# Moving the feed-forward weights' preparation and reordering the attention turns' seams in a fused transformer layer

## The chip, the cores and the metric

One core of one Trainium2 chip runs the whole program. The metric is device time in microseconds, taken as the median of the runs. The engines named below are TensorE (PE, matrix products), VectorE (DVE), ScalarE (ACT), GpSimd (POOL) and SyncE (SP, which issues most transfers). Each engine works through its own queue strictly in the order in which the program writes it, and waits on semaphores that other engines raise.

## The reference

```python
h = _layernorm(x) * (1 + ca) + sa            # x: (2, 1024, 256)
# 4 key/value heads, 4 query heads each, D = 128, causal
scores = einsum('bsgqd,btgd->bgqst', q, k) * scale
attn = softmax(where(causal, scores, -big))
x = x + ga * (einsum('bgqst,btgd->bsgqd', attn, v).reshape(b, s, NH*D) @ wproj)
h = _layernorm(x) * (1 + cb) + sb
h = fwht(h * SU_ug) / 64                     # Walsh-Hadamard transform, 256 wide
h = silu(h @ W_gate.T * g) * (h @ W_up.T * u)    # 1024 wide
x = x + gb * (fwht(h * SU_dp) / 64 @ W_down.T * d)
```

Everything is float32. The modulations (sa, ca, ga, sb, cb, gb) come from a small product of the conditioning vector.

## The kernel before

A float32 product is made of three reduced-precision products: each operand is split into a high part (rounded) and a low part (the rest), and `three()` issues high x high, high x low and low x high. So every operand needs a copy (the high part) and a subtraction (the low part) on ACT, DVE or POOL before PE may use it.

**Attention** runs in 8 turns t, one for each pair of batch and key/value head. The order of all work in it is one list, `WALK`, which every engine walks through, each taking its own share of each item:

- `C`: a chunk of the next turn's query, key or value projection; `S i h`: the scores of row block i (128 queries) and head part h, with the maximum on DVE, the exponential on ACT and the normalisation on POOL.
- `T n`: four transposes of unit n (a row block and a block of 128 keys), then the high part `pt_hi` on ACT and the low part `pt_lo` on DVE; `V n`: the product with the values, two units behind its T (`LAG`). After the last V of a row block ACT and DVE take `o_hi` and `o_lo` from the sum.
- `Y i`: the output projection of row block i (12 products), which DVE adds to x. `VS`: ACT and DVE split the next turn's values (`v_hi`, `v_lo`, two instructions each). `WP`: POOL splits the projection weights. `L`: PE transposes the second layer norm's input of two row blocks, with `LF`, `LN` before and `LH`, `LL` behind it.

Row blocks are worked in windows of a big and a small one: (7,0), (6,1), (5,2), (4,3). `UNITS` begins each window with three units (`HEAD`) of the big block, then takes the small one, then the rest of the big one. The **seam** is the stretch from turn t's last units to turn t+1's first transposes. Score tiles live in two pairs of PSUM banks, S[0] for h = 0 and 2, S[1] for h = 1 and 3. The scores of blocks 4 to 7 take a whole pair, so the wait ahead of them in PE's S branch (L1210 and L1211) is for the exponential of two score items earlier. The exponentials on ACT are put off by `exps()`: a score item's exponential is issued at ACT's next S, T, L or VS item. PE's two rotating transpose banks (`ring`) hold T and L tiles alike.

**The feed-forward part** folds the Walsh-Hadamard transforms into the weights. Six pieces, in the order `PIECES = [0, 1, 4, 5, 2, 3]` (0 to 3 up and gate, 4 and 5 down), each pass through: a sum and a difference on POOL (`last_butterfly`), a high part (`raw_hi`), a low part on POOL (`raw_lo`), four products with a Hadamard matrix `had_r` on PE (`P n`), and a high and a low part of the result on ACT and DVE (`weights_high`, `weights_low`). `split_piece(n)` does all POOL has to do of piece n at once. `B 2` in the last turn is piece 0; the others follow WALK. `FIRST` orders the first chunk of 512 rows: `G m` is gate and up product m (12 products), its silu, its product with the up half (`g32`) and the split into `g_hi` and `g_lo`; `D m` is the down product (12 products); `L n` a layer norm step. The other three chunks run in a loop.

Of the kernel before, what the change touches and what calls it, by code (L numbers as in the profile page):

```python
# [5 lines left out]
F32 = mybir.dt.float32  # L6
# [30 lines left out]
HEAD = 3  # L37
UNITS = []
for big, small in WINDOWS:
    UNITS += [(big, j) for j in range(HEAD)] + [(small, j) for j in range(small + 1)] + [(big, j) for j in range(HEAD, big + 1)]  # L40
# [33 lines left out]
def walk():  # L74
# [15 lines left out]
    for t in range(TURNS):  # L90
        s0, s6 = scores(t, 0), scores(t, NT - 2)
        rest = [(t - 1, "Y", i, 0) for i in WINDOWS[-1][::-1]] if t else []
        out += rest[:1] + [(t, "VS", 0, 0)] + s0[3 if t else 0:] + ([s6[0]] if t else []) + rest[1:]
# [13 lines left out]
        for p, pair in enumerate(WINDOWS):  # L107
# [64 lines left out]
def build(nc, x_in, wqkv, wv, wproj, wmod, c_cols, wug, wdn, su_ug, su_dp, ws_ug, ws_dp, ident_in, mask_in, had_in, out):  # L172
    ctx = ExitStack()
    with ctx:
# [337 lines left out]
        def _(pool):  # L512
# [67 lines left out]
            def split_piece(n):  # L580


                last_butterfly(PIECES[n])
                if n == 1:
                    pool.wait_ge(s_done, this(s_done, TURNS - 1, 32))
                if n < 4:
                    pool.wait_ge(last_fly_s, n + 1)
                    for k, z in enumerate(halves_of(PIECES[n])):
                        last = g_.tensor_scalar(raw_hi[n][:, k, :], z, 1.0, 1.0, ALU.mult, ALU.mult)
                    last.then_inc(rhi_s, 1)  # L590
# [33 lines left out]
            for t, what, n, h in WALK:  # L624
# [25 lines left out]
                if what == "B" and n == 2:  # L650
                    split_piece(0)
# [5 lines left out]
            for n in range(1, len(PIECES)):  # L657
                split_piece(n)
# [8 lines left out]
        def _(act):  # L667
# [94 lines left out]
            for t, what, n, h in WALK:  # L762
# [37 lines left out]
            def gated_high(m):  # L800

                act.wait_ge(g32_s, m + 3)
                a_.activation(g_hi[:, g_slot(m), :], g32[:, m % 2, :], ACT.Copy).then_inc(ghi_s, 1)

            for what, n in FIRST:
                if what == "P":
                    weights_high(n)
                if what == "P" and n in (2, 3):
                    raw_high(n + 2)
                if what == "G":  # L810
                    gate(0, n)
                    gated_high(n)
                if what == "L":
# [7 lines left out]
        def _(dve):  # L821
# [153 lines left out]
            for t, what, n, h in WALK:  # L975
# [394 lines left out]
```

## Time and profile before

| what | value |
|---|---|
| median of 3 runs | 945.65 us (945.41 to 945.97) |
| the profiled execution | 945.19 us, of which its span is 943.0 us |
| PE busy | 911.5 us, 97% of the span |
| DVE, ACT, POOL busy | 632.1, 511.3, 488.0 us |
| granted TensorE clock | 0.998 of full speed |
| PE, DVE, ACT, POOL over 820 to 900 us | 79.98, 45.36, 19.44, 6.56 us busy |

The span ends with the last store; the 2.2 us that the profiled execution has beyond it lie around it. Times in a timeline are from the span's start. A PE row is marked busy until its modelled end, which overlaps the next row: products of 512 columns follow one another 0.23 us apart though each is marked 0.39. So the start of one row to the start of the next is the safer measure of a wait.

### The profile page before, as it was taken

The page shows a single profiled execution, that of the slowest core. Times are in us where ns is not written, and L with a number is a line of the kernel's source. Part 1 is how long each engine was busy: PE and PEld are TensorE (multiplying, and loading weights), DVE is VectorE, ACT ScalarE, POOL GpSimd, SP SyncE. Part 2 cuts the span into 40 slices and gives each one's busy share as a digit, 9 for nine tenths or more (in the row PEclk, how much of TensorE's full clock was granted, in tenths as well). Part 3 has the DMA queues.
Part 4 walks back from the last instruction along what each step waited for, and adds up shares of the span by engine and source line. Part 5 has one row for each costly group of instructions (what it writes and reads, how often), then busy time and mean ns, then how long its engine had stood idle before and what let it go on. Part 6 is the DMA issues. An engine that isn't in the chain of part 4 may idle for free.

```text
span 943.0 us, 15013 instructions
## 1 busy us (share of the span) xinstructions
PE 911.5 (97%) x5480; PEld 805.4 (85%) x5480; DVE 632.1 (67%) x1299; ACT 511.3 (54%) x1113; POOL 488.0 (52%) x705
## 2 busy tenths in 40 slices
PE   5989999999999999999999999999999998899997
PEld 4878888888888888888888888888888987788886
DVE  6567757764787578747875787478757875664554
ACT  3366656654766476647664666476647664531111
POOL 2276718570767186707671867076717989420000
PEclk9999999999999999999999999999999999999999
DMA  7000100000001000000010000000001001000000
GB/s 278 23 1 1 41 1 23 1 28 1 23 1 40 1 23 1 28 1 23 2 40 1 23 1 29 2 17 7 1 1 68 1 30 45 1 12 11 22 22 23
DMA packets 10180, 21.21 MB, mean 22 GB/s; under 512 B 1280, under 2 KB 5760, under 8 KB 9984
## 3 DMA queue, kind: packets, MB, share of 16 engines
q1 hardware_dynamic: 9392, 20.11, 6.3%
q8 instruction: 41, 0.67, 0.3%
q10 hardware_dynamic: 720, 0.21, 0.1%
q14 instruction: 27, 0.22, 0.1%
HBM read 18.22 MB, written 2.10 MB: 22 GB/s over the span
## 4 chain that ended last, share of the span: by engine, by line
PE 71%; DVE 14%; ACT 7%; POOL 5%; issue 2%; DMA 1%; SPq 0%; DVEq 0%; POOLq 0%
PE ps L1089 16%; PE ps L1091 16%; PE ps L1090 16%; PE ps L1238 8%; DVE ps L1012 5%; PE ps L1227 5%; PE ps L1224 4%; PE ps L1221 4%; ACT prob L757 4%; DVE pt_lo L1016 3%; ACT pt_hi L782 2%; DVE stats L855 1%; DVE xhat L871 1%; PE ps L1113 1%; DVE vare L863 1%
## 5 line engine op out<-in xcount | busy, mean ns | idle before, releaser
L617 POOL TENSOR_TENSOR rinv<-rsum,mone 128x1 f32<-128x1 f32 x256 | 144.7, 565 | 243.3 <-ACT prob L757 243.3
L1016 DVE TENSOR_TENSOR pt_lo<-ps,pt_hi 128x512 fp32r<-128x512 f32 x288 | 198.0, 688 | 65.9 <-ACT pt_hi L782 62.8
L782 ACT ACTIVATE pt_hi<-ps 128x512 fp32r<-128x512 f32 x288 | 171.1, 597 | 126.5 <-PE ps L1238 126.0
L757 ACT ACTIVATE prob<-ps,nmax 128x256 f32<-128x256 f32 (+28 forms) x256 | 180.7, 706 | 85.2 <-DVE nmax L1012 84.2
L1012 DVE CUSTOM_DVE_ANT_0 ps<-ps,mask_f 128x256 f32<-128x256 f32 (+28 forms) x256 | 182.7, 719 | 46.8 <-PE ps L1227 44.7
L622 POOL TENSOR_SCALAR prob<-prob,rinv 128x256 f32<-128x256 f32 (+28 forms) x256 | 183.0, 715 | 38.2 <-POOL rinv L617 38.2
L1238 PE MATMUL ps<-ident,prob 128*128 128x128 f32 x1152 | 173.1, 273 | 4.5 <-POOL prob L622 2.7
L1238 PEld LDWEIGHTS ps<-ident,prob 128*128 128x128 f32 x1152 | 141.1, 141 | 23.5 <-DVE pt_lo L1016 3.7
L1089 PE MATMUL ps<-pt_hi,v_hi 128*128 128x512 f32 x288 | 134.5, 467 | 2.1 <-DVE pt_lo L1016 2.1
L1091 PE MATMUL ps<-pt_hi,v_lo 128*128 128x512 f32 x288 | 113.7, 395 | 0.0
L1090 PE MATMUL ps<-pt_lo,v_hi 128*128 128x512 f32 x288 | 113.5, 394 | 0.0
L1221 PE MATMUL ps<-k_hi,q_hi 128*128 128x256 f32 (+16 forms) x352 | 99.8, 343 | 0.6
L1227 PE MATMUL ps<-k_hi,q_lo 128*128 128x256 f32 (+16 forms) x352 | 98.0, 337 | 0.0
L1224 PE MATMUL ps<-k_lo,q_hi 128*128 128x256 f32 (+16 forms) x352 | 97.7, 337 | 0.0
L949 DVE SCALAR_TENSOR_TENSOR q_lo<-ps,q_hi 128x512 fp32r<-128x512 f32 x64 | 44.1, 691 | 55.4 <-ACT q_hi L722 55.4
L1221 PEld LDWEIGHTS ps<-k_hi,q_hi 128*128 128x128 f32 x352 | 62.9, 189 | 14.3 <-ACT prob L757 3.8
L1089 PE MATMUL ps<-wp_hi,o_hi 128*128 128x256 f32 x256 | 72.6, 284 | 0.0
L1091 PE MATMUL ps<-wp_hi,o_lo 128*128 128x256 f32 x256 | 72.4, 283 | 0.0
L1090 PE MATMUL ps<-wp_lo,o_hi 128*128 128x256 f32 x256 | 72.2, 282 | 0.0
L797 ACT ACTIVATE prob<-ps,ws_u 128x512 f32<-128x512 f32 x32 | 22.0, 688 | 86.8 <-PE ps L1091 86.8
L1224 PEld LDWEIGHTS ps<-k_lo,q_hi 128*128 128x128 f32 x352 | 63.9, 189 | 5.7
L1089 PE MATMUL ps<-h_hi,w_hi 128*128 128x512 f32 x160 | 66.0, 412 | 2.9 <-DVE h_lo L886 2.9
(173 smaller groups left out, 1794.9 us busy)
## 6 DMA issues: line engine op xcount, KB each, us to landing
w_raw<-in_wqkv SPq DMA_DIRECT2D x8, 640.0 KB, 3.9
wp_raw<-in_wproj SPq DMA_DIRECT2D x8, 512.0 KB, 3.4
out_y<-prob SPq DMA_DIRECT2D x8, 256.0 KB, 2.3
x<-in_x SPq DMA_DIRECT2D x3, 512.0 KB, 12.6
prob<-in_wug SPq DMA_DIRECT2D x3, 512.0 KB, 4.2
prob<-in_wmod SPq DMA_DIRECT2D x1, 1024.0 KB, 10.0
wv_raw<-in_wv SPq DMA_DIRECT2D x4, 256.0 KB, 4.4
raw_down<-in_wdn SPq DMA_DIRECT2D x1, 1024.0 KB, 4.8
```

The costliest lines, as they stand in the source:

```text
L622: g_.tensor_scalar(row(i, h), row(i, h), rinv[:, at, h:h + 1], 1.0, ALU.mult, ALU.mult).then_inc(prob_done, 1)
L757: a_.activation(row(i, h).rearrange("p (a n) -> p a n", a=nb), score_banks(i, h).rearrange("p (a n) -> p a n", a=nb)[:, :, 0:w], ACT.Exp, ...
L782: a_.activation(pt_hi[:, n % 3, :], ring(t, "T", n), ACT.Copy).then_inc(pth_done, 1)
L1012: v_.tensor_tensor_reduce(scores, scores, late, -1.0, 3.0e38, ALU.add, ALU.min, nmax[:, place(n), h:h + 1]).then_inc(max_done, 1)
L1016: v_.tensor_tensor(pt_lo[:, n % 3, :], ring(t, "T", n), pt_hi[:, n % 3, :].bitcast(F32), ALU.subtract).then_inc(ptl_done, 1)
L1089: mm(dst, w_h, r_h, start=start, stop=False)
L1090: mm(dst, w_h, r_l, start=False, stop=False)
L1091: return mm(dst, w_l, r_h, start=False, stop=stop)
L1221: mm(dst[:, a * CH:a * CH + wide], queries(q_hi, n, h), k_hi[:, a * w:a * w + wide], start=True, stop=False)
L1224: mm(dst[:, a * CH:a * CH + wide], queries(q_hi, n, h), k_lo[:, a * w:a * w + wide], start=False, stop=False)
L1227: last = mm(dst[:, a * CH:a * CH + wide], queries(q_lo, n, h), k_hi[:, a * w:a * w + wide], start=False, stop=True)
L1238: last = tr(ring(t, "T", n)[:, q * P:(q + 1) * P], row(i, q, j * P, (j + 1) * P), ident[:, :])
```

## The change

1. **Unit order and seams.** `HEADS` replaces HEAD: the last window begins with two units of block 4 instead of three, so block 3's last unit is unit 32 and no longer 33. `Y 3` (t) comes before S 0 1, S 0 2 (t+1) and V 35, and `Y 4` moves behind S 6 1, right before T 0. `L` moves behind the V item that followed it. On ACT two calls of exps() are left out, so that the exponential of S 7 3 goes behind pt_hi of unit 35.
2. **End of the last turn.** POOL does sums of later pieces ahead of low parts of earlier ones, and only the high part of piece 0 stays with it: ACT takes those of pieces 1, 2 and 3. The two Hadamard matrices' rounding moves from DVE to ACT. Both P 0 and P 1 come before Y 4.
3. **First chunk.** D m comes one gate later (behind G m+2), the splits of g32 get items `R` of their own, and g_hi, g_lo rotate over three slots.

```diff
-HEAD = 3
+HEADS = [3, 3, 3, 2]
...
-        rest = [(t - 1, "Y", i, 0) for i in WINDOWS[-1][::-1]] if t else []
-        out += rest[:1] + [(t, "VS", 0, 0)] + s0[3 if t else 0:] + ([s6[0]] if t else []) + rest[1:]
+        rest = [(t - 1, "Y", WINDOWS[-1][0], 0)] if t else []
+        out += [(t, "VS", 0, 0)] + s0[3 if t else 0:] + ([s6[0]] if t else [])
...
-                out += extra[:1] + [(t, "T", n, 0)] + extra[1:]
+                transposes = [item for item in extra if item[1] == "L"]
+                extra = [item for item in extra if item[1] != "L"]
+                out += extra[:1] + (rest if n == 0 else []) + [(t, "T", n, 0)] + extra[1:]
                 behind.append(n)
                 if len(behind) > LAG:
                     value()
+                out += transposes
...
-    for n, i in enumerate(WINDOWS[-1][::-1]):
-        out += [(TURNS - 1, "Y", i, 0), (TURNS - 1, "P", n, 0)]
+    out += [(TURNS - 1, "P", 0, 0), (TURNS - 1, "P", 1, 0), (TURNS - 1, "Y", WINDOWS[-1][0], 0)]
...
-FIRST = [("G", 0), ("P", 2), ("G", 1), ("D", 0), ("P", 3), ("G", 2), ("D", 1), ("P", 4), ("G", 3),
-         ("D", 2), ("P", 5), ("G", 4), ("D", 3), ("L", 0), ("G", 5), ("D", 4), ("L", 1), ("G", 6), ("D", 5), ("L", 2),
-         ("G", 7), ("L", 3), ("D", 6)]
+FIRST = [("G", 0), ("P", 2), ("R", 0), ("G", 1), ("P", 3), ("R", 1), ("G", 2), ("R", 2), ("D", 0), ("P", 4), ("G", 3), ("R", 3),
+         ("D", 1), ("P", 5), ("D", 2), ("G", 4), ("R", 4), ("D", 3), ("L", 0), ("G", 5), ("R", 5), ("D", 4), ("L", 1),
+         ("G", 6), ("R", 6), ("D", 5), ("L", 2), ("G", 7), ("R", 7), ("L", 3), ("D", 6)]
...
-            for n in range(1, len(PIECES)):
-                split_piece(n)
+            raw_low_part(0)
+            last_butterfly(PIECES[1])
+            last_butterfly(PIECES[2])
+            raw_low_part(1)
+            last_butterfly(PIECES[3])
+            raw_low_part(2)
+            raw_low_part(3)
+            last_butterfly(PIECES[4])
+            last_butterfly(PIECES[5])
+            raw_low_part(4)
+            raw_low_part(5)
...
                 if what == "S":
-                    exps()
+                    if not (t and n == h == 0):
+                        exps()
                     waiting.append((t, n, h))
...
-                    exps()
+                    if n != NU - 2:
+                        exps()
+                    if t == TURNS - 1 and n in (NU - 4, NU - 3):
+                        raw_high(1, n - NU + 4)
+                if what == "H":
+                    act.wait_ge(had_s, 16)
+                    for a in range(2):
+                        last = a_.activation(had_r[a], had_f[:, a, :], ACT.Copy)
+                    last.then_inc(consts, 1)
                 if what == "P":
                     weights_high(n)
+                    if n == 1:
+                        raw_high(3)
...
+                    if t == TURNS - 1 and n == NU - 1:
+                        raw_high(2)
```

What the queues hold, in the order in which the instructions stand, with the semaphores they wait for. First ACT's queue at a seam, before: from the exponential of S 7 3 (1024 wide) to that of S 0 3 (128 wide); 32, 64, 96 and 128 columns are S 0 0 to S 0 3.

```order
L757 ACTIVATE prob,rsum<-ps,nmax 128x1024 [waits max_done]
L782 ACTIVATE pt_hi<-ps 128x512 [waits transposed]
L757 ACTIVATE prob,rsum<-ps,nmax 128x32 [waits max_done]
L789 ACTIVATE o_hi<-ps 128x512 [waits pv_done]
L757 ACTIVATE prob,rsum<-ps,nmax 128x64 [waits max_done]
L789 ACTIVATE o_hi<-ps 128x512 [waits pv_done]
L757 ACTIVATE prob,rsum<-ps,nmax 128x96 [waits max_done]
L704 ACTIVATE v_hi<-raw_down 128x512 [waits pv_done,v_raw_done]
L704 ACTIVATE v_hi<-raw_down 128x512
L757 ACTIVATE prob,rsum<-ps,nmax 128x128 [waits max_done]
```

And the same place now:

```order
L816 ACTIVATE o_hi<-ps 128x512 [waits pv_done]
L799 ACTIVATE pt_hi<-ps 128x512 [waits transposed]
L773 ACTIVATE prob,rsum<-ps,nmax 128x1024 [waits max_done]
L773 ACTIVATE prob,rsum<-ps,nmax 128x32 [waits max_done]
L773 ACTIVATE prob,rsum<-ps,nmax 128x64 [waits max_done]
L816 ACTIVATE o_hi<-ps 128x512 [waits pv_done]
L773 ACTIVATE prob,rsum<-ps,nmax 128x96 [waits max_done]
L716 ACTIVATE v_hi<-raw_down 128x512 [waits pv_done,v_raw_done]
L716 ACTIVATE v_hi<-raw_down 128x512
L773 ACTIVATE prob,rsum<-ps,nmax 128x128 [waits max_done]
```

The first `o_hi` (block 3) and a `pt_hi` moved ahead of the 1024-wide exponential. The exponential of S 0 2 (96) still stands behind `o_hi` of block 4, which waits for V 35, and that of S 0 3 (128) behind both `v_hi`.

PE's queue at the same seam, before, from S 0 1 to the first transpose of the next turn (`wp_hi,o_hi` is a Y item, `pt_hi,v_hi` a V item; the first row of each is shown, "..." stands for its others):

```order
L1217 MATMUL ps<-k_first,q_first 128x64 [waits first_row_done,exp_done]
L1217 MATMUL ps<-k_first,q_first 128x96 [waits first_row_done,exp_done]
L1089 MATMUL ps<-pt_hi,v_hi 128x512 [waits pt_lo_done]
...
L1089 MATMUL ps<-wp_hi,o_hi 128x256 [waits o_lo_done]
...
L1217 MATMUL ps<-k_first,q_first 128x128 [waits first_row_done,exp_done]
L1221 MATMUL ps<-k_hi,q_hi 128x400 [waits exp_done]
...
L1089 MATMUL ps<-wp_hi,o_hi 128x256 [waits o_lo_done]
...
L1221 MATMUL ps<-k_hi,q_hi 128x416 [waits exp_done]
...
L1238 MATMUL ps<-ident,prob 128x128 [waits prob_done,pt_lo_done]
```

And now:

```order
L1124 MATMUL ps<-pt_hi,v_hi 128x512 [waits pt_lo_done]
...
L1124 MATMUL ps<-wp_hi,o_hi 128x256 [waits o_lo_done]
...
L1252 MATMUL ps<-k_first,q_first 128x64 [waits first_row_done,exp_done]
L1252 MATMUL ps<-k_first,q_first 128x96 [waits first_row_done,exp_done]
L1124 MATMUL ps<-pt_hi,v_hi 128x512 [waits pt_lo_done]
...
L1252 MATMUL ps<-k_first,q_first 128x128 [waits first_row_done,exp_done]
L1256 MATMUL ps<-k_hi,q_hi 128x400 [waits exp_done]
...
L1256 MATMUL ps<-k_hi,q_hi 128x416 [waits exp_done]
...
L1124 MATMUL ps<-wp_hi,o_hi 128x256 [waits o_lo_done]
...
L1273 MATMUL ps<-ident,prob 128x128 [waits prob_done,pt_lo_done]
```

Y 3 moved from between V 35 and S 0 3 (128x128) to ahead of S 0 1, and Y 4 from between S 6 0 (400) and S 6 1 (416) to behind both.

DVE's queue at the same seam now holds, from the addition of Y 3 on, the maxima (ISA), `o_lo` and the values' low parts:

```order
L1051 TENSOR_TENSOR x<-ps,x 128x256 [waits y_done]
L1037 ISA ps,nmax<-ps,mask_f 128x64 [waits scores_done]
L1037 ISA nmax 128x1
L1037 ISA ps,nmax<-ps,mask_f 128x96 [waits scores_done]
L1037 ISA nmax 128x1
L1046 TENSOR_TENSOR o_lo<-ps,o_hi 128x512 [waits o_hi_done]
L985 TENSOR_TENSOR v_lo<-raw_down,v_hi 128x512 [waits v_hi_done] x2
L1037 ISA ps,nmax<-ps,mask_f 128x128 [waits scores_done]
L1037 ISA nmax 128x1
L1037 ISA ps,nmax<-ps,mask_f 128x2x400 [waits scores_done]
L1037 ISA nmax 128x1
```

The addition of Y 3 stands ahead of the maxima of S 0 1 and S 0 2, where it used to stand behind `o_lo`; the maximum of S 0 3 stands behind both `v_lo`, as before.

Last, ACT's queue at the end of the last turn, from unit 29's high part to the first weights' high parts (`su_u`), before:

```order
L782 ACTIVATE pt_hi<-ps 128x512 [waits transposed] x7
L789 ACTIVATE o_hi<-ps 128x512 [waits pv_done] x2
L730 ACTIVATE q_hi<-ps,su_u 128x512 [waits hadamard_done] x4
```

And now:

```order
L799 ACTIVATE pt_hi<-ps 128x512 [waits transposed] x3
L807 ACTIVATE had_r<-prob 128x128 [waits had_loaded]
L807 ACTIVATE had_r<-prob 128x128
L799 ACTIVATE pt_hi<-ps 128x512 [waits transposed]
L760 ACTIVATE k_hi<-dif_down 128x512 [waits scores_done,last_butterflies]
L799 ACTIVATE pt_hi<-ps 128x512 [waits transposed]
L760 ACTIVATE k_hi<-prob 128x512 [waits scores_done,last_butterflies]
L799 ACTIVATE pt_hi<-ps 128x512 [waits transposed]
L816 ACTIVATE o_hi<-ps 128x512 [waits pv_done]
L799 ACTIVATE pt_hi<-ps 128x512 [waits transposed]
L816 ACTIVATE o_hi<-ps 128x512 [waits pv_done]
L760 ACTIVATE q_hi<-sum_down 128x512 [waits last_butterflies]
L760 ACTIVATE q_hi<-raw_down 128x512
L742 ACTIVATE q_hi<-ps,su_u 128x512 [waits hadamard_done] x4
```

ACT's queue gained the two `had_r` rows (from DVE), and `k_hi` and `q_hi` of pieces 1 and 2 (from POOL). The last two `q_hi` rows stand ahead of the four weights' rows for which the first gate product waits.

## Rows read from the trace of the kernel before

**Rows 1.** The page: busy times by engine, and one costly group (busy, mean ns, idle).

```profile
PE 911.5 (97%) x5480; PEld 805.4 (85%) x5480; DVE 632.1 (67%) x1299; ACT 511.3 (54%) x1113; POOL 488.0 (52%) x705
...
L617 POOL TENSOR_TENSOR rinv<-rsum,mone 128x1 f32<-128x1 f32 x256 | 144.7, 565 | 243.3 <-ACT prob L757 243.3
```

**Rows 2.** PE's waits: who was waited for, total us, times, longest.

```profile
PE ps L1113 <- DVE pt_lo L1016: 2.3, 8, 0.3
PE ps L1089 <- DVE pt_lo L1016: 2.1, 7, 0.4
```

**Rows 3.** Timeline of PE at turn 6's seam: start, us, operation.

```profile
713.68 0.58 PE L1217 MATMUL ps<-k_first,q_first 128*128 128x64 f32 x4
...
714.54 0.50 PE L1089 MATMUL ps<-pt_hi,v_hi 128*128 128x512 f32 x1 [0.28 <-DVE pt_lo L1016]
...
715.34 0.34 PE L1089 MATMUL ps<-wp_hi,o_hi 128*128 128x256 f32 x1
...
716.98 0.60 PE L1221 MATMUL ps<-k_hi,q_hi 128*128 128x400 f32 x2
...
718.15 0.28 PE L1089 MATMUL ps<-wp_hi,o_hi 128*128 128x256 f32 x1
...
719.58 0.54 PE L1221 MATMUL ps<-k_hi,q_hi 128*128 128x416 f32 x2
...
720.71 0.60 PE L1238 MATMUL ps<-ident,prob 128*128 128x128 f32 x4
```

**Rows 4.** Timeline of ACT at the same seam.

```profile
715.77 0.59 ACT L789 ACTIVATE o_hi<-ps 128x512 fp32r<-128x512 f32 x1
716.25 0.34 ACT L757 ACTIVATE prob<-ps,nmax 128x96 f32<-128x96 f32 x1
...
716.57 1.16 ACT L704 ACTIVATE v_hi<-raw_down 128x512 fp32r<-128x512 f32 x2
718.96 0.37 ACT L757 ACTIVATE prob<-ps,nmax 128x128 f32<-128x128 f32 x1 [1.24 <-DVE nmax L1012]
719.23 0.19 ACT L757 ACTIVATION_READ_ACCUMULATOR prob<-ps,nmax 128x1 f32 x1
```

**Rows 5.** Timeline of DVE at the same seam.

```profile
717.38 1.28 DVE L955 TENSOR_TENSOR v_lo<-raw_down,v_hi 128x512 fp32r<-128x512 f32 x2
...
718.58 0.29 DVE L1012 CUSTOM_DVE_ANT_0 ps<-ps,mask_f 128x128 f32<-128x128 f32 x1
```

**Rows 6.** Timeline of POOL at the same seam.

```profile
717.43 1.04 POOL L617 TENSOR_TENSOR rinv<-rsum,mone 128x1 f32<-128x1 f32 x1
```

**Rows 7.** Timeline of PE around item L of turn 6.

```profile
655.33 0.60 PE L1238 MATMUL ps<-ident,prob 128*128 128x128 f32 x4
...
656.23 0.66 PE L1113 MATMUL ps<-ident,xhat 128*128 128x128 f32 x4 [0.30 <-DVE pt_lo L1016]
...
657.90 0.60 PE L1238 MATMUL ps<-ident,prob 128*128 128x128 f32 x4
```

**Rows 8.** Timeline of DVE at that place.

```profile
656.77 0.69 DVE L1016 TENSOR_TENSOR pt_lo<-ps,pt_hi 128x512 fp32r<-128x512 f32 x1
```

**Rows 9.** Timeline of PE, last turn and first chunk: the four long waits.

```profile
778.97 0.33 PE L1238 MATMUL ps<-ident,prob 128*128 128x128 f32 x1 [1.09 <-POOL prob L622]
...
786.14 0.66 PE L1238 MATMUL ps<-ident,prob 128*128 128x128 f32 x4 [1.31 <-DVE pt_lo L1016]
...
802.88 0.39 PE L1089 MATMUL ps<-k_hi,pt_hi 128*128 128x256 f32 x1 [1.50 <-DVE v_lo L970]
...
820.01 0.39 PE L1089 MATMUL ps<-k_hi,pt_hi 128*128 128x256 f32 x1 [1.61 <-DVE pt_lo L1037]
```

**Rows 10.** Timeline of POOL in the last turn.

```profile
772.05 1.29 POOL L593 TENSOR_TENSOR w_lo<-dif_down,w_hi 128x512 fp32r<-128x512 f32 x1
```

**Rows 11.** Timeline of DVE in the last turn.

```profile
783.14 2.34 DVE L989 CAST had_r<-prob 128x128 fp32r<-128x128 f32 x2
```

**Rows 12.** Timeline of ACT: the first weights' high parts.

```profile
792.25 1.27 ACT L730 ACTIVATE q_hi<-ps,su_u 128x512 fp32r<-128x512 f32 x2 [1.31 <-PE ps L1188]
```

More of the change, by code:

```diff
@@ L36 @@
 WINDOWS = [(NT - 1 - p, p) for p in range(NW)]
-HEAD = 3
+HEADS = [3, 3, 3, 2]
 UNITS = []
-for big, small in WINDOWS:
-    UNITS += [(big, j) for j in range(HEAD)] + [(small, j) for j in range(small + 1)] + [(big, j) for j in range(HEAD, big + 1)]
+for (big, small), ahead in zip(WINDOWS, HEADS):
+    UNITS += [(big, j) for j in range(ahead)] + [(small, j) for j in range(small + 1)] + [(big, j) for j in range(ahead, big + 1)]
 NU = len(UNITS)
@@ L142, in walk @@
             value()
-        assert [i for _, i in due] == list(WINDOWS[-1][::-1])
-    for n, i in enumerate(WINDOWS[-1][::-1]):
-        out += [(TURNS - 1, "Y", i, 0), (TURNS - 1, "P", n, 0)]
+        assert [i for _, i in due] == [WINDOWS[-1][0]]
+    out += [(TURNS - 1, "P", 0, 0), (TURNS - 1, "P", 1, 0), (TURNS - 1, "Y", WINDOWS[-1][0], 0)]
     return out
@@ L578, in last_butterfly, with first_high, raw_low_part @@
                 g_.tensor_tensor(b, a, b, ALU.subtract).then_inc(last_fly_s, 1)
[L580 to L590, printed above, removed]
+            def first_high():
+                pool.wait_ge(last_fly_s, 1)
+                for k, z in enumerate(halves_of(PIECES[0])):
+                    last = g_.tensor_scalar(raw_hi[0][:, k, :], z, 1.0, 1.0, ALU.mult, ALU.mult)
+                last.then_inc(rhi_s, 1)
+            def raw_low_part(n):
                 pool.wait_ge(rhi_s, n + 1)
@@ L737, in weights_high, with raw_high @@
                         last.then_inc(fhi_s, 1)
-            def raw_high(n):
+            def raw_high(n, only=None):
                 act.wait_ge(last_fly_s, n + 1)
+                if n == 1:
+                    act.wait_ge(s_done, this(s_done, TURNS - 1, 32))
                 if n == 4:
@@ L744, in raw_high @@
                 for k, z in enumerate(halves_of(PIECES[n])):
-                    last = a_.activation(raw_hi[n][:, k, :], z, ACT.Copy)
-                last.then_inc(rhi_s, 1)
+                    if only in (None, k):
+                        last = a_.activation(raw_hi[n][:, k, :], z, ACT.Copy)
+                if only != 0:
+                    last.then_inc(rhi_s, 1)
             waiting = []
@@ L807, in _ @@
                     weights_high(n)
-                if what == "P" and n in (2, 3):
-                    raw_high(n + 2)
                 if what == "G":
                     gate(0, n)
+                if what == "R":
                     gated_high(n)
+                    if n < 2:
+                        raw_high(n + 4)
                 if what == "L":
@@ L985, in _ @@
                         ln_low(0, 0, 1, slot)
-                if what == "H":
-                    dve.wait_ge(had_s, 16)
-                    for a in range(2):
-                        last = v_.tensor_copy(had_r[a], had_f[:, a, :])
-                    last.then_inc(consts, 1)
                 if what == "G":
@@ L1032, in gated, with gated_high, gated_low, product @@
                                         ALU.mult, ALU.mult).then_inc(g32_s, 1)
+            def gated_high(c, m):
                 dve.wait_ge(g32_s, c * NM + m + 3)
[L1034 to L1035 removed]
+                v_.tensor_copy(g_hi[:, g_slot(m), :], g32[:, m % 2, :]).then_inc(ghi_s, 1)
+            def gated_low(c, m, first=False):
                 dve.wait_ge(ghi_s, c * NM + m + 1)
[L1037 removed]
+                v_.tensor_tensor(g_lo[:, g_slot(m, first), :], g32[:, m % 2, :], g_hi[:, g_slot(m, first), :].bitcast(F32),
                                  ALU.subtract).then_inc(g_ok, 1)
+            def product(c, m):
+                gated(c, m)
+                gated_high(c, m)
+                gated_low(c, m)
             def scale_out(c):
@@ L1061, in _ @@
                 if what == "G":
-                    gated(0, n, False)
+                    gated(0, n)
+                if what == "R":
+                    gated_low(0, n, True)
                 if what == "L":
@@ L1069, in _ @@
             with dve.Fori(1, B * NC_B) as c:
-                gated(c, 0)
+                product(c, 0)
                 scale_out(c - 1)
-                gated(c, 1)
+                product(c, 1)
                 finish(c - 1)
                 for m in range(2, NM):
-                    gated(c, m)
+                    product(c, m)
             scale_out(B * NC_B - 1)
@@ L1281, in gate_up, with down @@
                 last.then_inc(gu_s, 1)
-            def down(c, m):
+            def down(c, m, first=False):
                 if m == 0:
@@ L1308, in _ @@
                         pe.wait_ge(wf_ok, KH * (PIECES.index(4 + n // 2) + 1))
-                    down(0, n)
+                    down(0, n, True)
                 if what == "L":
```

19 lines of the change are left out of this document (10 added, 9 removed).

## The prediction

> **What bounds the kernel now.** The page first: PE is busy 911.5 us, 97% of the span [rows 1]. Whatever helps another engine counts only where PE waits for it, so I read next who PE waits for. Apart from the start and the last store there are few places. Two come in every turn: the transposes of item L wait for `pt_lo` (8 times, 2.3 us together), and the value product V 35 at the seam waits for it (7 times, 2.1 us) [rows 2]. Four come once, at the end of the last turn and in the first chunk: 1.09 us for POOL's scores, 1.31 for `pt_lo`, 1.50 for `v_lo`, 1.61 for the low part of g [rows 9]. With the tails that are marked busy ahead of them (0.15 to 0.35 each) the four are 6.3 us; a fifth of 0.19 (no row here) makes it 6.5. So the most that the change can win, if it removes all of it and adds nothing, is 6.5 us there, 8 x 0.54 at L, and 7 x 0.6 at the seam: about 15 us. What it costs depends on the waits that it lays bare, so each place has to be walked through with PE's starts.
>
> **The seams.** In turn 6's seam PE starts S 0 1 at 713.68, V 35 at 714.54, Y 3 at 715.34, S 6 0 at 716.98, Y 4 at 718.15, S 6 1 at 719.58 and T 0 at 720.71 [rows 3]. Without a wait S 0 1 and S 0 2 would take 0.28 (their row is marked 0.58, of which some 0.3 is tail), so V 35 lost 0.58 there. The pieces of work are then, start to start: V 35 0.80, Y 3 1.50, S 0 3 0.14 (together 1.64 up to S 6 0), S 6 0 1.17, Y 4 1.43, S 6 1 1.13.
>
> Now put them in the new order, from the same 713.68. Y 3 runs to 715.18 (its `o_lo` is early, since block 3 ends one unit sooner), S 0 1 and S 0 2 to 715.46, V 35 to 716.26 without its wait, S 0 3 to 716.40. S 6 0 must have the exponential of S 0 2. On ACT that stands behind `o_hi` of block 4, which needs V 35. Before, `o_hi` began at 715.77, 0.43 after V 35, but behind another exponential; alone I take 0.20 (between nothing and 0.43). Then, from ACT's starts [rows 4], 0.48 for `o_hi` and 0.32 for the exponential with a tail of 0.1 until it is seen. That is 716.26 + 0.20 + 0.48 + 0.42 = 717.36 to 717.4. So S 6 0 waits 1.0 us where it used to wait for nothing: Y 3, which stood between V 35 and it, is gone.
>
> S 6 1 needs the exponential of S 0 3. It stands behind both `v_hi`, and its maximum behind both `v_lo`. From the first `v_hi` (716.57) to that exponential (718.96) took 2.39, and it ended 0.46 later at 719.42 [rows 4]. DVE's two `v_lo` (717.38) and the maximum (718.58) lie inside it [rows 5]. Of the 2.39 a part was `v_lo` beginning 0.2 late behind Y 3's addition, which now comes earlier, so I take 2.2 to 2.39. The new `v_hi` begins at 717.26, so the exponential ends at 719.9 to 720.1 and S 6 1 starts at about 720.0. S 6 0 was done at 717.4 + 1.17 = 718.57: a wait of 1.4 us. In the kernel before, 1.43 us of Y 4 lay exactly there, and S 6 1 began 0.16 after the exponential's end [rows 3, 4]. Now Y 4 comes behind S 6 1 and T 0 starts at 720.0 + 1.13 + 1.43 = 722.56 instead of 720.71. **Each seam loses 1.85 us, seven of them 13.0.** Check by waits: 1.0 + 1.4 new, 0.58 gone. Bounds: 1.6 (no latency after V 35, 2.2) to 2.1 (0.43, 2.39). The exponential of S 7 3, now behind `pt_hi` of unit 35, ends some 0.8 us later; S 0 1, which needs it, starts 1.5 later than it did, so this costs nothing.
>
> **Item L.** The transposes end at 655.69 (655.33 and 0.36) and L begins at 656.23, 0.54 late [rows 7]. With V 12 (0.77) between them L no longer waits. The next transposes (657.90) need unit 14's `pt_lo`, which ends at 656.77 + 0.69 = 657.46 and does not depend on L [rows 7, 8]. They can move up only to 657.5. So 0.38 of the 0.54 is won, 8 x 0.38 = 3.1 us (bounds 2.4 and 4.3).
>
> **The end of the last turn and the first chunk.** Term by term:
> - The 1.09 (1.44 with its tail): the transposes of block 3 wait for the scores' normalisation, behind four instructions of piece 0. The two of the low part take 2.5 us from 772.05 on [rows 9, 10] and move behind. The same transposes come 1.13 us earlier. 0.1 is left: 1.3 won.
> - The 1.31 (1.48): DVE rounds the Hadamard matrices in 2.34 us from 783.14 on, ahead of a `pt_lo` [rows 9, 11]. On ACT they lie in a gap of some 0.9 us. No row shows this copy on ACT; it is no more than the 512 wide `v_hi` (0.58 each) [rows 4], so 0.4 to 1.2 us, hidden but for at most 0.3. All of it is won. But block 3's first value product now follows block 5's projection by one transposes item (0.35) and shares its bank, so it waits for an addition on DVE: 0.2 + 0.42 + 0.06 less 0.35 = 0.33 lost.
> - POOL's new order delivers piece 1's sums at 781.4, and ACT takes its halves between two `pt_hi`. No wait of PE follows.
> - The first gate product needs the weights of piece 0. ACT now does both halves of piece 2 (about 1.05) before their high parts, which take 1.27 [rows 12], then 0.7 for the last low part. PE reaches the product 0.65 before that: 0.65 lost.
> - The 1.50 and 1.61 (3.4 with tails): down product 0 now stands behind gate 2, 3.6 us more of cover, and D 3 has its g one gate earlier on PE's side. The layer norm's 4.1 us on DVE still stand before g 3, but begin 5 us sooner. 0.25 is left.
>
> 6.5 less 0.1, 0.33, 0.65 and 0.25 is 5.2 us won (bounds 4.0 and 6.5). From 820 us on PE was full and stays so.
>
> **A rule against it.** DVE's two `v_lo` read two SBUF tensors each. While they ran, POOL's one-column reciprocal took 1.04 us, where its mean is 0.565 [rows 1, 6]. The Trainium skill (SBUF — State Buffer, "SBUF: two separate sides") says that GpSimd and a VectorE instruction with two SBUF inputs take a shared port pair in turn, and that whichever comes second is fully blocked. By that rule, the trace agrees. Before, the second `v_lo` came first; in the new seam POOL's scores of S 0 2 fall due just before it, and if POOL is first the chain to S 6 1 grows by up to 0.5 us, seen from the 0.48 by which that reciprocal was longer. I leave it out of the sum and keep it as a rival.
>
> **The sum**, against the profiled execution's 945.19 us: + 13.0 - 3.1 - 5.2 = + 4.7, so 949.9. The median of the runs lies 0.46 above that execution; I say 950.0. Own range: + 11.2 - 4.3 - 6.5 = + 0.4 to + 14.7 - 2.4 - 4.0 = + 8.3, that is 946.0 to 954.0 on the median's scale.
>
> **The rivals.**
> - *Forecast, slower by 3 to 8 us:* 0.62.
> - *POOL is first at the shared port:* 7 x 0.5 more, about 953.5. For it the 1.04 us; against it, the two start within a tenth of each other, so either may win. 0.13.
> - *The seams' waits are as costed at the low end and the other gains at the high end, or one of the waits is smaller by 0.5 us:* within 0.2% (1.9 us, about what a measurement of this kernel can tell from no change) of before. 0.13.
> - *Faster:* the seam is not bound by ACT's queue, S 6 0 and S 6 1 find their exponentials done, and the 0.58 of V 35 is won: 945.65 - 4.1 - 3.1 - 5.2 = 933.3. For it, that Y 3 ahead of S 0 1 is just what removes the one wait that the seam shows [rows 3]. Against it, both queues in order: the exponential of S 0 2 can't pass `o_hi`, nor that of S 0 3 the `v_hi`. The point that decides is a seam that loses under (3.1 + 5.2) / 7 = 1.2 us. 0.12.
>
> Range, with the near parts of the neighbouring cases: 945.0 to 954.5. Slower by over 0.2% (above 947.5): 0.77; within 0.2%: 0.12; faster: 0.11.
>
> **What would show it.** In the new trace: S 6 0 (400 columns) and S 6 1 (416) each preceded by an idle PE released by ACT's `prob`, about 0.8 and 1.2 us idle, seven times, and no wait at the 128x64 score rows or V 35; L's transposes without one; from the end of V 35 to T 0 6.3 us instead of 5.4. In the last turn, the four long waits gone, and ones of about 0.3 and 0.65 before the first value product of block 3 and the first gate product. I am wrong if the seam is short (then the first part of this text failed), or if ACT in the last turn holds up `pt_hi` behind a sum that POOL has not finished.

## The result and the profile after

The changed kernel takes **957.87 us** (median of 4 runs, 957.75 to 958.36) against 945.81 for the kernel before on the same chip: ratio 1.0126, 95% interval 1.0113 to 1.0139. The forecast was 950.0 with a range up to 954.5. It has the direction and is off by 8 us in size. The profiled execution took 957.75 (span 955.9, against 943.0). The mean granted clock was 0.988 to 0.991 in all four executions, where those of the kernel before that are on record with a clock have 0.995 to 0.998.

The page after, the lines that answer to [rows 1], and the granted clock's line:

```profile
PE 918.4 (96%) x5480; PEld 811.3 (85%) x5480; DVE 629.8 (66%) x1297; ACT 516.6 (54%) x1121; POOL 489.7 (51%) x699
...
PEclk9999999999999999999999999999999999999999
```

PE is *busier* by 6.9 us with the same 5480 matmuls. So the loss is not idle time alone: some products took longer. The clock's line hides why, since a slice is 24 us and a digit 9 stands for anything from 90% up. PE's waits after (who was waited for, total us, times, longest):

```profile
PE ps L1256 <- ACT prob L773: 14.3, 14, 1.3
...
PE ps L1222 <- POOL w_lo L595: 0.7, 1, 0.7
PE ps L1124 <- issue: 0.5, 1, 0.5
PE ps L1124 <- DVE o_lo L1046: 0.2, 1, 0.2
```

L1256 is the first product of a score block. It waits for ACT's exponentials 14 times, twice in each of seven seams. The waits of [rows 2] and the four of [rows 9] are gone; the wait of 0.2 for `o_lo` is one of turn 1 alone. PE at turn 6's seam, answering to [rows 3]:

```profile
729.55 0.58 PE L1252 MATMUL ps<-k_first,q_first 128*128 128x64 f32 x4
729.91 0.47 PE L1124 MATMUL ps<-pt_hi,v_hi 128*128 128x512 f32 x1
...
731.86 0.45 PE L1256 MATMUL ps<-k_hi,q_hi 128*128 128x400 f32 x1 [0.79 <-ACT prob L773]
...
734.47 1.06 PE L1256 MATMUL ps<-k_hi,q_hi 128*128 128x416 f32 x2 [1.25 <-ACT prob L773]
735.33 0.89 PE L1259 MATMUL ps<-k_lo,q_hi 128*128 128x416 f32 x2
736.02 0.90 PE L1262 MATMUL ps<-k_hi,q_lo 128*128 128x416 f32 x2
736.72 0.41 PE L1124 MATMUL ps<-wp_hi,o_hi 128*128 128x256 f32 x1
736.93 0.42 PE L1125 MATMUL ps<-wp_lo,o_hi 128*128 128x256 f32 x1
...
738.68 0.60 PE L1273 MATMUL ps<-ident,prob 128*128 128x128 f32 x4
```

Up to the start of S 6 1 this is the forecast seam: V 35 without a wait, S 6 0 1.95 us after V 35, S 6 1 2.61 behind it. Then it is not. S 6 1's next two groups begin 0.86 and 0.69 later; at full clock the block's three groups take 1.13 in all [rows 3]. Y 4's products stand 0.21 apart instead of 0.12 (1.43 for twelve), until 737.9. The windows of PE (span, busy and count, granted clock, DMA share, GB/s) show it in turn 1's seam, which is built alike:

```profile
249.00:251.00 2.00, 1.15 (x3) 0.70 0.00 0
251.00:253.00 2.00, 2.00 (x9) 0.50 0.00 0
253.00:255.00 2.00, 2.00 (x16) 0.95 0.00 0
```

A granted clock of 0.50 is 1.2 GHz. It fell at the end of the second wait (the first products behind it start at 249.85) and came back some 3.4 us later; no DMA was moving here, so it isn't traffic. In turn 3's seam, with the same two waits, it stayed:

```profile
445.00:447.00 2.00, 0.91 (x5) 1.00 0.00 0
447.00:449.00 2.00, 2.00 (x18) 1.00 0.00 0
```

Seam by seam, from the first product of S 7 0 to T 0 (each duration is the difference of two starts in PE's timeline):

| seam of turn | 0 | 1 | 2 | 3 | 4 | 5 | 6 | sum |
|---|---|---|---|---|---|---|---|---|
| before | 18.84 | 18.96 | 18.85 | 18.85 | 18.85 | 18.84 | 18.85 | 132.0 |
| after | 20.83 | 22.87 | 22.37 | 20.85 | 22.37 | 20.84 | 22.38 | 152.5 |

The rest of the 12.9 us, in the same way: between the seams -2.0, up to turn 0's first T item -0.5, from T 0 of the last turn to the end 222.3 to 217.2, -5.1. With +20.5 from the seams that is +12.9.

ACT at turn 6's seam, answering to [rows 4]:

```profile
730.89 0.60 ACT L816 ACTIVATE o_hi<-ps 128x512 fp32r<-128x512 f32 x1
731.38 0.34 ACT L773 ACTIVATE prob<-ps,nmax 128x96 f32<-128x96 f32 x1
...
731.70 0.63 ACT L716 ACTIVATE v_hi<-raw_down 128x512 fp32r<-128x512 f32 x1
733.96 0.37 ACT L773 ACTIVATE prob<-ps,nmax 128x128 f32<-128x128 f32 x1 [1.11 <-DVE nmax L1037]
```

`o_hi` follows V 35's end (729.91 + 0.78) by the 0.20 that the prediction took, and the first exponential ends 0.14 before S 6 0 starts. The second begins 2.26 after the first `v_hi`, inside the prediction's 2.2 to 2.39.

### The profile page after: what moved, and what is told of

Its sections match the earlier page's. It is cut to its first block, busy times and chain, and to the rows that moved or that the text cites. A ratio compares the mean times of both kernels' runs of the same rounds, so it can differ in the third digit from the quotient of the medians.

```text
span 955.9 us, 15006 instructions
## 1 busy us (share of the span) xinstructions
PE 918.4 (96%) x5480; PEld 811.3 (85%) x5480; DVE 629.8 (66%) x1297; ACT 516.6 (54%) x1121; POOL 489.7 (51%) x699
## 4 chain that ended last, share of the span: by engine, by line
PE 80%; DVE 9%; ACT 6%; issue 2%; POOL 2%; DMA 0%; DVEq 0%; SPq 0%; POOLq 0%; ACTq 0%
PE ps L1124 18%; PE ps L1126 17%; PE ps L1125 17%; PE ps L1273 11%; PE ps L1256 5%; PE ps L1262 5%; PE ps L1259 5%; ACT prob L773 3%; DVE ps L1037 3%; ACT pt_hi L799 2%; DVE pt_lo L1041 2%; DVE v_lo L985 1%; DVE stats L885 1%; PE ps L1148 1%; DVE vare L893 1%
## 5 line engine op out<-in xcount | busy, mean ns | idle before, releaser
L619 POOL TENSOR_TENSOR rinv<-rsum,mone 128x1 f32<-128x1 f32 x256 | 141.5, 553 | 251.6 <-ACT prob L773 251.0
L624 POOL TENSOR_SCALAR prob<-prob,rinv 128x256 f32<-128x256 f32 (+28 forms) x256 | 190.0, 742 | 38.2 <-POOL rinv L619 38.2
L1256 PE MATMUL ps<-k_hi,q_hi 128*128 128x256 f32 (+16 forms) x352 | 102.7, 351 | 14.9 <-ACT prob L773 14.3
L1256 PEld LDWEIGHTS ps<-k_hi,q_hi 128*128 128x128 f32 x352 | 63.3, 191 | 32.0 <-ACT prob L773 21.9
```

Of the source, the lines that this page charges most:

```text
L624: g_.tensor_scalar(row(i, h), row(i, h), rinv[:, at, h:h + 1], 1.0, ALU.mult, ALU.mult).then_inc(prob_done, 1)
L1256: mm(dst[:, a * CH:a * CH + wide], queries(q_hi, n, h), k_hi[:, a * w:a * w + wide], start=True, stop=False)
```

## The experiments

Names used again: **y_back** is the changed kernel with the seams' Y 3 and Y 4 at their old places, and **pieces** is y_back without item L's move, the later down products and the Hadamard rounding on ACT.

**seams_only**: the kernel before with the seams' edits (the new `HEADS` and `rest`, and the exponentials' order on ACT).

> The kernel before with the seams' edits alone (order of units, Y3 ahead of S 0 1, Y4 behind S 6 1, the exponentials' order); item L, the end of the last turn and the first chunk as before. Theory A (the seams' two waits, and the fall of the granted clock to 1.2 GHz that they bring in four of seven seams, are all of the loss): +20 us, about 965 to 966. Theory B (waits alone come from the seams, 2.0 us each, and the low clock comes from something else in the change): +14, about 960. Theory C (the loss needs the other edits too): below 955.

Measured 965.15 (ratio 1.0199, 1.0182 to 1.0216). Theory A's number, though not by its sum alone: the seven seams lost 18.7 us, three of them fell to 1.2 GHz (22.70, 22.29 and 22.36 us) and four stayed at 20.83 to 20.85. Another 3.4 came in the last turn and the first chunk of the profiled execution (966.73, the longest of the four; the others took 965.10 to 965.19). There the new order of units, without the other moves, waits twice for POOL's scores (1.02 and 1.09), 0.51 for `o_lo` and 2.08 for g's low part, and behind that last wait the clock fell once more:

```profile
839.99 0.39 PE L1090 MATMUL ps<-k_hi,pt_hi 128*128 128x256 f32 x1 [2.08 <-DVE pt_lo L1038]
```

```profile
840.00:842.00 2.00, 2.00 (x11) 0.64 0.00 0
```

Theory B falls: the low clock needs nothing but the seams' edits. C falls as well.

**y_back**:

```
-        rest = [(t - 1, "Y", WINDOWS[-1][0], 0)] if t else []
-        out += [(t, "VS", 0, 0)] + s0[3 if t else 0:] + ([s6[0]] if t else [])
+        rest = [(t - 1, "Y", i, 0) for i in WINDOWS[-1][::-1]] if t else []
+        out += rest[:1] + [(t, "VS", 0, 0)] + s0[3 if t else 0:] + ([s6[0]] if t else []) + rest[1:]
...
```

(The lines left out keep Y 3 and Y 4 from being issued at the changed kernel's places as well.)

> The changed kernel with the projections Y3 and Y4 at the places of the kernel before, so that 1.5 and 1.4 us of products stand again ahead of S 6 0 and S 6 1; all else is the change. Theory A: the seams go back to 18.9 us each or a little less, the clock stays at 1.00, and what is left of the change is its gains: 945.8 - 0.35 - 2.2 - 5.1 = 938 (937 to 939.5). Theory C: the loss comes with the new order of units or of the exponentials, and stays: over 950.

Measured **938.89** (0.9926, 0.9909 to 0.9942): seams of 18.92 (turn 1's 19.03), the clock at 1.00 in all of them. Two projections' places are worth 19 us. V 35's wait is gone here too, but the seams are no shorter than before (18.85): S 0 1 now waits 0.39 for the exponential of S 7 3, which the change put behind a `pt_hi`. The prediction's reason why that costs nothing, a later S 0 1, holds only with Y 3 ahead of it.

**y4_between**: `... + ([s6[0]] if t else []) + rest`, and `rest` no longer ahead of T 0.

> The changed kernel with Y4 back between S 6 0 and S 6 1, Y3 still ahead of S 0 1: the first wait (about 1.0 us) stays, the second (1.25) goes. Theory A, if the clock falls only where both waits come: seams of 18.85 + 1.0 - 0.6 = 19.3 us, sum 938.2 + 7 x 0.4 = 941, clock 1.00 in all seams. Theory A, if one wait of 1 us suffices: 941 + 6 = 947 with 1.2 GHz stretches still there. Theory C: over 950.

Measured 942.5 (0.9963, 0.9949 to 0.9977). Seams of 19.40 (turn 1's 19.90), S 6 0 waiting 0.8 us in each of the seven, and PE's windows of turn 1's seam read

```profile
246.00:248.00 2.00, 2.00 (x13) 1.00 0.00 0
248.00:250.00 2.00, 2.00 (x15) 1.00 0.00 0
```

The first wait alone did not bring the clock down.

**fill** and **fill_first**: the changed kernel with extra products ahead of S 6 0 and S 6 1, or ahead of S 6 0 alone (`h < 1`).

```
                     elif e <= QPG and not t:
                         pe.wait_ge(*evicted(t, 9))
+                    if t and n == NT - 2 and h < 2:
+                        for _ in range(4 + h):
+                            mm(ring(t, "T", 0), k_hi[:, 0:P], k_hi[:, 0:CH], start=True, stop=True)
                     if e > 2:
                         pe.wait_ge(exp_done, ...)
```

> The changed kernel with four extra products (k_hi by k_hi, 512 columns) just ahead of S 6 0 and five ahead of S 6 1, in turns 1 to 7. Their results go to a bank that T 0 overwrites; nothing else uses them. TensorE then works through most of both waits, and the waits' ends stay where ACT puts them. If the low clock is what idle TensorE brings: no row of the seams under 0.95, each seam 20.8 us as the three undisturbed ones, 957.9 - 6.5 = 951.4 (950.5 to 952.5). If the slow rows behind the waits have another cause (the moved Y4, its operands, traffic): no change, 957 to 960.

> The changed kernel with the four extra products ahead of S 6 0 alone (their results are overwritten by T 0 and used nowhere); the wait of 1.25 us ahead of S 6 1 stays idle. y4_between showed the other half: the wait ahead of S 6 0 alone never brought the clock down. If it takes both waits within three us: all seams at 20.8 (the turn 2 one 21.4), no clock row under 0.95, 951.5 to 952.5. If the second wait suffices by itself: 955 to 958 with 1.2 GHz in some seams.

Measured 952.16 (fill) and 952.15 (fill_first). In both, six seams take 20.83 to 20.85 and turn 1's 21.3 to 21.4, and in none of them the clock falls. fill has 63 *more* products than the changed kernel and is 5.7 us faster; its timeline shows five of them in the second gap, and S 6 1's groups again 0.48 and 0.38 apart:

```profile
728.94 1.32 PE L1247 MATMUL ps<-k_hi 128*128 128x512 f32 x5
730.35 0.65 PE L1259 MATMUL ps<-k_hi,q_hi 128*128 128x416 f32 x2
730.83 0.54 PE L1262 MATMUL ps<-k_lo,q_hi 128*128 128x416 f32 x2
731.21 0.53 PE L1265 MATMUL ps<-k_hi,q_lo 128*128 128x416 f32 x2
```

With the first gap filled and the second idle (fill_first), turn 1's seam keeps its clock too:

```profile
249.00:251.00 2.00, 1.44 (x7) 1.00 0.00 0
251.00:253.00 2.00, 1.30 (x7) 1.00 0.00 0
```

So the slow products come from what idles ahead of them. One of these two gaps alone, the first (y4_between) or the second (fill_first), brought no fall in seven seams each; both brought four in seven and three in seven. That is not so of every lone gap: the one of 2.08 in seams_only had a fall behind it.

**scores_first**: the changed kernel with `scores(t + 1, 0)[1:4]` ahead of Y 3 and V 35, and `exps()` ahead of block 4's `o_hi`.

> The changed kernel with the scores S 0 1, S 0 2 and S 0 3 together ahead of Y3 and V 35, and ScalarE's exponentials of them ahead of the high part of block 4's output; Y4 stays behind S 6 1. If the two waits of the seams come from the order of ScalarE's queue, as the prediction said (the exponentials stand behind the high parts that need V 35): both waits go or fall under 0.3 us, seams of 18.9 to 19.4, 938.5 to 942. If they come from the work between (VectorE's low parts and maxima): a wait of over 0.8 us stays, 945 or more.

Measured 944.01 (0.9979, 0.9969 to 0.9989), 2 us over the expected range. Both waits go and the seams are 18.94, so ACT's order is what S 6 0 and S 6 1 wait for. But the wait turns up one item later. S 6 2 comes 1.15 behind T 0, where y_back has 0.36:

```profile
724.63 0.60 PE L1278 MATMUL ps<-ident,prob 128*128 128x128 f32 x4
725.78 0.66 PE L1261 MATMUL ps<-k_hi,q_hi 128*128 128x432 f32 x2 [0.55 <-ACT prob L776]
```

ACT shows which exponential it is, that of S 6 0, and what is late:

```profile
721.66 1.14 ACT L719 ACTIVATE v_hi<-raw_down 128x512 fp32r<-128x512 f32 x2
724.71 0.93 ACT L776 ACTIVATE prob<-ps,nmax 128x800 f32<-128x800 f32 x1 [1.90 <-DVE nmax L1042]
```

The high and low parts that the exponentials were moved past now stand ahead of S 6 0's maximum and exponential. Seven times 0.8 is 5.6, the distance to y_back by the two profiled spans (942.5 less 936.9); by the medians it is 5.1.

**y3_split**: y_back with Y 3's first two heads ahead of S 0 1 (`range(2 * h, 2 if what == "YH" else QPG)`).

> The kernel y_back with Y3 cut in two: its first two heads (0.74 us of products) ahead of S 0 1, its last two between V 35 and S 6 0, where all of it stood. The first half covers V 35's wait for its low part (0.6 us), the second still covers most of the wait that the changed kernel had ahead of S 6 0. Reading by the changed kernel's chain (S 6 0 can start 2.05 us after V 35 starts): V 35 starts at most 0.2 later, S 6 0 0.2 to 0.3 us earlier, clock 1.00: seams of 18.65 to 18.75 us, 937.0 (936.5 to 938). If what S 6 0 waits for is late by more: no gain, 938.5 to 940.

Measured **937.93** (0.9918, 0.9904 to 0.9931), the fastest of all, faster than both kernels. Six of its seams are 18.77, 0.15 shorter than y_back's, and turn 1's is 0.24 longer (19.27), 0.7 in all; between the two medians alone the difference would not be told from noise.

**l_only**:

```
+                transposes = [item for item in extra if item[1] == "L"]
+                extra = [item for item in extra if item[1] != "L"]
                 out += extra[:1] + [(t, "T", n, 0)] + extra[1:]
 ...
+                out += transposes
```

> The kernel before with item L alone moved behind the value product. Theory A (each L wins 0.28 to 0.38 us, eight times, and nothing follows): 946.0 - 2.3 to 3.0, so 943 to 943.7; no idle TensorE ahead of L's transposes. Rival (the next transposes were what bounded, and L's wait was free): within 1 us of before.

Measured 943.12 (0.9973, 0.9962 to 0.9984). Each turn is 0.32 shorter.

**d_early** and **h_dve**: y_back with one step undone each, `FIRST`'s down products one gate earlier, or the `had_r` copies on DVE.

> The kernel y_back with the down products of the first chunk one gate earlier again (down product 0 behind gate 1, 1 behind gate 2, 2 behind gate 3), all other moves of GpSimd and ScalarE kept. If the later place is what wins the 3.15 us that the prediction gave it: 938.9 + 2.5 to 3.4, about 942, with waits for v_lo or the low part of g back. If the earlier low parts from GpSimd and the separate rounding would have done it alone: 939 to 940.

> The kernel y_back with the rounding of the Hadamard matrices back on VectorE. The prediction gave its move to ScalarE 1.48 us. If that is so: 940.4 (939.9 to 940.9), and a wait of about 1.3 us for pt_lo at a transposes item of the last turn. If ScalarE's queue paid for it: 939 or less.

Measured 939.58 (0.9931, 0.9916 to 0.9947) and 939.18 (0.9928, 0.9913 to 0.9944), which can't be told from y_back's 0.9926. Only the traces separate them: by the profiled stretch from T 0 of the last turn to the end (y_back 217.15 us) they are 0.5 and 1.1 longer. d_early waits 0.45 and 0.23 for g, h_dve 0.79 for `pt_lo`. Neither step has the size that the prediction gave it, 3.15 and 1.48.

**d_only** and **pieces**: the later down products alone, and the edits that are left.

> The kernel before with the first chunk's down products one gate later (and the third slot of g that this needs), nothing else. The prediction's term (the 1.50 and the 1.61 us with their tails go, by the place alone): 945.6 - 3.2 = 942.5. By d_early, where the earlier place cost 0.5 to 0.7 us: most of the two waits was not the place's to win; then the wait of 1.61 ahead of down product 3, whose place hardly moves, stays, and it is 943.8 to 945.6.

> What is left of the change without its seams (Y3 and Y4 at their old places), item L's move, the later down products and the Hadamard matrices on ScalarE: GpSimd's sums ahead of its low parts, the high parts on ScalarE, the gate products' rounding as items of their own, the last window's order. From the single steps (y_back 938.9, + 0.6 for the down products, + 0.7 for the Hadamard matrices, + 2.4 for L): 942.6 (942 to 943.3), so 3 us won with no wait for v_lo over 0.5 us ahead of down product 0. By the prediction's terms (it gave these edits 1.3 - 0.33 - 0.65 = 0.3 us): 945.3.

Measured 946.05 (1.0001, 0.9992 to 1.0011) and 943.07 (0.9968, 0.9956 to 0.9979). In d_only the 1.50 ahead of down product 0 is gone, and stands ahead of the next weights' Hadamard product instead. The low part of the weights that it waited for is no earlier, and PE needs it at the next item:

```profile
803.44 0.47 PE L1187 MATMUL ps<-q_hi,had_r 128*128 128x512 f32 x1 [1.64 <-DVE v_lo L970]
...
820.48 0.39 PE L1089 MATMUL ps<-k_hi,pt_hi 128*128 128x256 f32 x1 [0.82 <-DVE pt_lo L1037]
```

The pieces' edits win 2.9 by themselves.

**sums_behind** and **r_joined**: pieces with POOL's loop `last_butterfly(PIECES[n]); raw_low_part(n)` again, and pieces with each `("R", m)` right behind its `("G", m)` in `FIRST`.

> The kernel pieces with GpSimd's sums one by one ahead of their own low part again, as in the kernel before; only the place of piece 0's low part, behind the last scores, is kept. If the sums' new order is what brings the weights earlier to the first chunk: 943.1 + 1 to 2.5, with the wait for w_lo or v_lo back at the gate or down products. If ScalarE's high parts and the place of piece 0's low part do it: 943 to 943.6.

> The kernel pieces with the rounding of each gate product (R) right behind its gate (G) again on ScalarE and VectorE, ahead of the next weights' high parts. If the separate rounding is what lets the weights of the next piece come earlier: 943.1 + 0.5 to 2. If not: 943.1 or a little less, since the down products get their g sooner (the waits of 0.45 and 0.25 for pt_lo shrink).

Measured 946.24 (1.0005, 0.9996 to 1.0014) and 946.97 (1.0014, 1.0005 to 1.0023): either step back takes all of the 2.9 away, and more than was expected of it (3.2 and 3.9 us more than pieces, for 1 to 2.5 and 0.5 to 2). Down product 0, which waits 0.45 in pieces, waits here (sums_behind first, r_joined in the second fence):

```profile
805.18 0.35 PE L1116 MATMUL ps<-k_hi,pt_hi 128*128 128x256 f32 x1 [3.35 <-DVE pt_lo L1057]
```

```profile
803.92 0.58 PE L1121 MATMUL ps<-k_hi,pt_hi 128*128 128x256 f32 x1 [3.39 <-DVE v_lo L992]
```

ACT's timeline has both reasons. In sums_behind it waits 2.84 for a sum of POOL, with the first gate's work and its rounding (802.83) queued behind:

```profile
798.26 0.63 ACT L752 ACTIVATE q_hi<-sum_down 128x512 fp32r<-128x512 f32 x1 [2.84 <-POOL raw_down L581]
```

In r_joined the down weights' high parts (`k_hi`) stand behind a piece that waits for POOL, where pieces has them ahead of it, at 800.12:

```profile
800.30 0.63 ACT L757 ACTIVATE w_hi<-dif_down 128x512 fp32r<-128x512 f32 x1 [1.16 <-POOL prob L579]
...
801.36 0.82 ACT L744 ACTIVATE k_hi<-ps,su_d 128x256 fp32r<-128x256 f32 x2
```

So the gain needs both edits. In the profiled execution of r_joined the wait isn't all: the clock was at 0.50 from 803.1, during the wait, to 810.0. From down product 0 to the end it took 2.6 us more than pieces (141.7 for 139.1), though its later wait is only 0.1 longer. sums_behind waited as long and kept its clock at 1.00. r_joined's window behind the wait:

```profile
804.00:806.00 2.00, 2.00 (x9) 0.50 0.00 0
```

## Why the prediction was off, step by step

- **The sum itself** is + 4.7 on the profiled execution. On the median's scale that is 950.35 and not the 950.0 that the text then says, and 8 x 0.38 is 3.04 for its 3.1; neither slip matters beside what follows.
- **The seams' waits** (1.0 and 1.4, so 1.85 a seam): right in place, releaser and chain, and close in size. In the seams at full clock the loss is 1.99 (20.84 less 18.85), seven times 13.9 for the 13.0 forecast. Of the 0.14, 0.11 lies behind S 6 1's start: it took 2.67 from there to T 0 for the 2.56 of the sum.
- **The step that failed** is "T 0 starts at 720.0 + 1.13 + 1.43": the work behind the waits was priced at the durations of a seam without gaps. In four of seven seams PE's granted clock fell to 1.2 GHz behind the second wait, and the same products took 1.53 more (22.37 less 20.84), 6.1 in all. The bounds, 1.6 to 2.1 a seam, varied only ACT's times, so no end of the range held this. fill shows it: with the gaps worked through, the seams sum to 6.1 less. The trace before had the price. At turn 0's first scores PE has three gaps near each other, and the block of 400 columns behind them takes 2.16 (56.34 to 58.50) where turn 6's takes 1.17 [rows 3]. The prediction didn't look there:

```profile
51.82 0.41 PE L1217 MATMUL ps<-k_first,q_first 128*128 128x32 f32 x2 [1.14 <-ACT prob L757]
53.30 0.94 PE L1217 MATMUL ps<-k_first,q_first 128*128 128x64 f32 x6 [1.07 <-ACT prob L757]
...
56.13 0.48 PE L1238 MATMUL ps<-ident,prob 128*128 128x128 f32 x1 [1.57 <-POOL prob L622]
56.34 1.03 PE L1221 MATMUL ps<-k_hi,q_hi 128*128 128x400 f32 x2
...
58.50 0.96 PE L1238 MATMUL ps<-ident,prob 128*128 128x128 f32 x4
```

```profile
56.30:59.20 2.90, 2.90 (x11) 0.50 0.00 0
```

- Turn 1's seam lost 0.4 to 0.5 more than the others wherever Y 3, or half of it, stands ahead of S 0 1: in the changed kernel, seams_only, y4_between, fill, fill_first and y3_split. In y_back it is 0.1 longer than the others, as before. Y 3 waits there for `o_lo`, in front of which DVE has a `gb_row` multiplication in this turn. This is read from the trace; no run took that instruction away:

```profile
241.93 0.69 DVE L969 TENSOR_TENSOR gb_row<-gb_row,ws_row 128x512 f32<-128x512 f32 x1
242.65 0.69 DVE L1046 TENSOR_TENSOR o_lo<-ps,o_hi 128x512 fp32r<-128x512 f32 x1
```

```profile
243.39 0.38 PE L1124 MATMUL ps<-wp_hi,o_hi 128*128 128x256 f32 x1 [0.23 <-DVE o_lo L1046]
```

- **Item L**: the mechanism right, the size 0.32 for 0.38, 2.5 us for 3.1.
- **The last turn and the first chunk**: the sum nearly right (5.1 with one L of 0.3 in it, so 4.8 for 5.2), its terms not, when they are tried one by one. The later down products were given 3.15 and win nothing alone, 0.5 as the last step. The edits on POOL and ACT, given 0.3, win 2.9 together, and none of it if one of two is missing. The Hadamard rounding wins 1.1 for 1.48, by one trace of each kernel. The error was to subtract a cover from a wait without asking who else needs the late tile.
- **The two small losses of that stretch** came as forecast: block 3's first value product starts 0.68 behind its transposes where the units behind it take 0.35 to 0.36, 0.33 late, and gate product 0 starts 0.70 late for 0.65. The page marks that gap "issue", but PE's instruction there waits for the second low part of piece 0's weights, and DVE ended it (809.49 + 0.74) 0.10 before. Not foreseen is the wait of 0.67 behind down product 0, where the Hadamard product of the fifth piece waits for POOL's low part:

```profile
809.49 1.40 DVE L995 SCALAR_TENSOR_TENSOR q_lo<-ps,su_u,q_hi 128x512 fp32r<-128x512 f32 x2
```

```profile
810.33 0.47 PE L1124 MATMUL ps<-h_hi,q_hi 128*128 128x512 f32 x1 [0.55 <-issue]
...
822.66 0.50 PE L1222 MATMUL ps<-w_hi,had_r 128*128 128x512 f32 x1 [0.67 <-POOL w_lo L595]
```

- **POOL first at the shared port**: did not happen. S 6 1 came as costed, and POOL's 64-column scores, 0.16 behind the start of DVE's two `v_lo`, took 1.24, until 0.11 behind the second one's end (732.36 + 1.29). So it went in six of the seven seams; in turn 1's the same row was done before the first `v_lo` (247.74) and took 0.32, and S 6 1 came no earlier or later there (2.61 behind S 6 0):

```profile
732.52 1.24 POOL L624 TENSOR_SCALAR prob<-prob,rinv 128x64 f32<-128x64 f32 x1
```

```profile
247.39 0.32 POOL L624 TENSOR_SCALAR prob<-prob,rinv 128x64 f32<-128x64 f32 x1
```

  Where the two met, DVE was first, and POOL paid. The rule of the Trainium skill (SBUF — State Buffer, "SBUF: two separate sides"), that the second of the two is fully blocked, agrees with the first row. No run put POOL first, so what that would have cost stays open.
- **Faster** and **within noise**: not so. The point set for them, a seam that loses under 1.2 us, is passed on the other side.

## What to carry to other kernels

A product that doesn't depend on a chain is worth most where it lies ahead of the item that ends the chain: Y 3 moved forward removed a wait of 0.6 and laid bare one of 1.0, and half of it moved does both jobs. Where two new gaps come close together on TensorE, add the products behind them at half clock as the upper bound of the sum, and look in the trace at hand for a stretch at the lower clock and what idled ahead of it. Before a wait is booked as won by more cover, look for the next reader of the same late tile: if PE needs it one item later, only an earlier tile helps.

## What was not expected of the hardware

Two gaps of TensorE of 1.0 and 1.4 us (0.79 and 1.25 marked idle), with 1.2 us of products between them, sufficed for a fall of the granted clock to 0.50 for about 3.4 us, in 4 of 7 seams and, with the same seams in another kernel, in 3 of 7. Either of the two alone brought none in its seven seams. Which seam falls differs between the two kernels (1, 2, 4, 6 and 1, 2, 6); the traces don't show what decides it.

Longer lone gaps went either way. Marked idle, one of 2.08 (seams_only) had a fall of 3.4 us behind it and during one of 3.39 (r_joined) began a fall of 6.8; those of 1.50 and 1.61 (the kernel before) and of 3.35 (sums_behind) had none. The three gaps at turn 0's first scores had one in the trace of every kernel here: 3.4 us long in four of them, 6.8 in the others. So idle time by itself doesn't tell whether the clock falls, and the half-clock price is a bound and not a forecast.

A kernel with 63 extra products was 5.7 us faster than the one without.
